# Graph attention: the quarter of the messages that ScalarE weighed is weighed by GpSimd, in the queue that gathers

## The chip, the cores and the metric

The kernel runs on one core of a Trainium2 chip. The metric is the device time of one execution in microseconds (us). TensorE is called PE here (PEld is its loading of weights), VectorE DVE, ScalarE ACT, GpSimd POOL and SyncE SP, as in the profile.

## The reference, cut to what matters

The program is a two-layer graph network over 3125 nodes with 256 features and 53125 edges sorted by their target node. The change touches the first layer's graph attention alone (8 heads of 32 columns):

```python
q = (x @ Wq + bq).reshape(n, H, C)
k = (x @ Wk + bk).reshape(n, H, C)
v = (x @ Wv + bv).reshape(n, H, C)
alpha = jnp.einsum('ehc,ehc->eh', q[dst], k[src]) / jnp.sqrt(jnp.float32(C))
amax = jax.ops.segment_max(alpha, dst, num_segments=n)
ex = jnp.exp(alpha - amax[dst])
denom = jax.ops.segment_sum(ex, dst, num_segments=n)
attn = ex / denom[dst]
msg = (v[src] * attn[:, :, None]).reshape(-1, H * C)
out = jax.ops.segment_sum(msg, dst, num_segments=n)
```

The kernel sums `v[src] * ex` and `ex` by target and divides later. The multiplication of the 256 columns of v[src] by their head's ex is what is called weighing below.

## The kernel before

`attention` (L887) walks over 440 steps (T1) of 128 edges each. Four steps are a half (Q4), two steps a pair (the code says duo), eight a unit U, sixteen a batch (B16); there are 110 halves and 27.5 batches. All targets of a step lie in one block of 128 nodes, so sums by target are matmuls with a one-hot matrix. The engines run their own queues, written out by hand, and meet at semaphores. Every queue is in order: what stands behind a wait waits as well.

**POOL (L943 to L952)** gathers the k and v rows of each step, 128 rows of 2 KB from `kv_tab` in DRAM, into the ring `kv`, which has 32 slots (RING * Q4), two batches. Before the gather of step t it waits until PE has summed step t - 32 (`summed`), whose slot it overwrites, and until DVE has multiplied about up to step t - 12 (`multiplied`).

**PE (`fetch`, L1057; `attend`, L1076)** spreads the targets' q rows over the edges of a pair (L1072, bf16, six matmuls) and counts `asked`. `attend` sums a pair: one matmul with zeros clears the second bank (L1083), then it waits for the one-hot of the half (`built`) and for the half's weighing, and multiplies (L1097, two f32 passes for each step, so four records a pair); each step counts `summed`. In a batch it also transposes scores and maxima (L1119, L1130) and makes small matmuls for the state carried from batch to batch (L1124, L1127, L1133). The order in the loop over batches (L1105 on) is fixed: pairs 1 to 8 of the batch before lie among the q matmuls of the coming one, and the transposition of the scores is behind all eight.

**DVE (L1135 on)** multiplies q by the gathered k rows (L1154, 128x512 for a pair), reduces by head (L1161, a half), adds the sums of a pair to the accumulator (L1181), and runs the segmented maximum by scans (L1243 to L1261). It ends a batch's scores with a subtraction of the maxima (L1267, `diffed`), which releases ACT's exponentials. It weighs three halves of each batch, 0, 1 and 3, at L1170 with one multiplication of 128x1024 each:

```python
v.tensor_tensor(rows, rows, wide(kv[:, slot(hh), 2 * D:2 * D + H1].unsqueeze(3), [P, Q4, H1, HD]),
                ALU.mult).then_inc(weighted, 1)
```

Its order around the place in question is add of pair 4, multiply, weighing of half 3, **add of pair 5**, reduction, add of pair 6, two multiplications, reduction, adds of pairs 7 and 8, scans, and the subtraction at L1267.

**ACT (L978 on)** makes the one-hot matrices: `node_hot` in bf16 for the q matmuls (L991, L994) and `edge_hot` in f32 for the sums (four times L1010, then L1015, counted by `built`). In a batch it first exponentiates (L1036, four times L1040, counted by `exped`), then in this order: `edge_hot` of half 1, weighing of steps 0 and 1 of half 2, `node_hot`, weighing of steps 2 and 3 of half 2, `edge_hot` of half 2, `node_hot`, `edge_hot` of half 3, `node_hot`, `edge_hot` of the next half 0, `node_hot`. The weighing is `weigh` (L1017 to L1026): one activation with a scale by partition for each step and head, 32 of 128x32 for a half (L1025). PE waits for it before pairs 5 and 6, by `weighed`.

**SP** loads the rows of targets and the flags.

Of the kernel before, what the change touches and what calls it, by code (L numbers as in the profile page):

```python
# [10 lines left out]
ALU = mybir.AluOpType  # L11
ACT = mybir.ActivationFunctionType
AX = mybir.AxisListType

P = 128
N = 3125
D = 256
# [12 lines left out]
T1 = C1 + NB - 1  # L30
G1 = (T1 + P - 1) // P
H1 = 8
# [67 lines left out]
def wide(ap, shape):  # L100
    return ap.to_broadcast(shape)
# [779 lines left out]
Q4 = U // 2  # L881
B16 = 2 * U
RING = 8
# [3 lines left out]
def attention(nc, k, e, q_parts, kv_tab, acc):  # L887
# [3 lines left out]
    HD = D // H1  # L891
    W = D + H1
    SCALE = float(HD ** -0.5)
    halves, duos = T1 // Q4, T1 // 2
    batches = -(-T1 // B16)
    NHOT, NEDGE, NROW = 4, 3, 4
    with Scope(nc) as s:
        kv = s.sb("at_kv", [P, RING * Q4, 2 * D + H1])
# [35 lines left out]
        weighed = s.sem("at_weighed")  # L934

        def slot(hh):
            return slice(hh % RING * Q4, hh % RING * Q4 + Q4)

        def halves_of(j):
            return list(range(4 * j, min(4 * j + 4, halves))) if 0 <= j < batches else []  # L940

        with nc.Block(no_gpsimd_drain=True) as block:
            @block.gpsimd  # L943
            def _(pool):
                for t in range(T1):
                    if t >= RING * Q4:
                        pool.wait_ge(summed, t - RING * Q4 + 1)
                    if t >= AHEAD + 2:
                        pool.wait_ge(multiplied, (t - AHEAD) // 2)
                    nc.gpsimd.indirect_dma_start(  # L950
                        out=kv[:, t % (RING * Q4), 0:2 * D], out_offset=None, in_=kv_tab,
                        in_offset=bass.IndirectOffsetOnAxis(ap=e.src[:, t:t + 1], axis=0)).then_inc(got[t // Q4 % RING], 16)  # L952

            @block.sync
            def _(sp):
# [22 lines left out]
            @block.scalar  # L978
            def _(act):
                a = nc.scalar.activation  # L980
                made = [0]

                def node_hot(hh):
                    if hh >= halves:
                        return
                    act.wait_ge(rowed[hh // 2 % (NROW // 2)], 16 * (hh // NROW + 1))
                    if hh:
                        act.wait_ge(hotted, hh)
                    if hh >= NHOT:
                        act.wait_ge(asked, 2 * (hh - NHOT) + 2)  # L990
                    a(away_n[:, :], rel_row[:, hh % NROW, :], ACT.Abs, bias=k.neg_col[:, :]).then_inc(away, 1)  # L991
                    made[0] += 1
                    act.wait_ge(away, made[0])
                    a(hot_n[:, hh % NHOT, :], away_n[:, :], ACT.Relu, bias=k.ones[:, 0:1], scale=-1.0).then_inc(hotted, 1)  # L994

                def first(j):
                    if j >= batches:
                        return
                    act.wait_ge(hotted, 4 * j + 1)
                    if j >= 3:  # L1000
                        act.wait_ge(rescaled, j - 2)
                    a(first_hot[:, j % 2:j % 2 + 1], hot_n[:, 4 * j % NHOT, 0:1], ACT.Copy).then_inc(firsted, 1)

                def edge_hot(hh):
                    if hh >= halves:
                        return
                    if hh:
                        act.wait_ge(built, hh)
                    for u in range(Q4):
                        a(away_e[:, u, :], k.count_row[:, 0:P], ACT.Abs, bias=e.rel[:, hh * Q4 + u:hh * Q4 + u + 1], scale=-1.0).then_inc(away, 1)  # L1010
                    made[0] += Q4
                    act.wait_ge(away, made[0])
                    if hh >= NEDGE:
                        act.wait_ge(summed, (hh - NEDGE + 1) * Q4)
                    a(hot_e[:, hh % NEDGE], away_e[:, :, :], ACT.Relu, bias=k.ones[:, 0:1], scale=-1.0).then_inc(built, 1)  # L1015

                def weigh(j, us):  # L1017
                    hh = 4 * j + 2
                    if hh >= halves:
                        return  # L1020
                    act.wait_ge(exped, hh + 1)
                    for u in us:
                        for h in range(H1):
                            row = kv[:, hh % RING * Q4 + u, D + h * HD:D + (h + 1) * HD]
                            ins = a(row, row, ACT.Copy, scale=kv[:, hh % RING * Q4 + u, 2 * D + h:2 * D + h + 1])  # L1025
                        ins.then_inc(weighed, 1)  # L1026

                for x in range(4):
                    node_hot(x)
                edge_hot(0)  # L1030
                for x in range(4, 8):
                    node_hot(x)
                for j in range(batches):
                    if j:
                        act.wait_ge(fell, j)
                        a(fade[:, j % 2:j % 2 + 1], fall[:, j % 2:j % 2 + 1], ACT.Exp, scale=SCALE).then_inc(faded, 1)  # L1036
                    act.wait_ge(diffed, j + 1)
                    for x, hh in enumerate(halves_of(j)):
                        act.wait_ge(got[hh % RING], 16 * Q4 * (hh // RING + 1))
                        a(kv[:, slot(hh), 2 * D:W + D], below[:, x * Q4:(x + 1) * Q4, :], ACT.Exp, scale=SCALE).then_inc(exped, 1)  # L1040
                    first(j + 1)
                    edge_hot(4 * j + 1)
                    weigh(j, (0, 1))
                    node_hot(4 * j + 8)
                    weigh(j, (2, 3))
                    edge_hot(4 * j + 2)
                    node_hot(4 * j + 9)
                    edge_hot(4 * j + 3)
                    node_hot(4 * j + 10)
                    edge_hot(4 * j + 4)  # L1050
                    node_hot(4 * j + 11)

            @block.tensor
            def _(pe):
# [21 lines left out]
                def attend(j, *xs):  # L1076
                    for x in xs:
                        p = j * U + x
                        if j < 0 or p >= duos:
                            continue  # L1080
                        if p >= 2:
                            pe.wait_ge(added, p - 1)
                        nc.tensor.matmul(ps_a[p % 2][:, 1, 0:W], nothing[:, 0:P], nothing[:, :], start=True, stop=False, skip_group_check=True)  # L1083
                        pe.wait_ge(built, p // 2 + 1)
                        if p // 2 % 4 == 2:
                            pe.wait_ge(weighed, Q4 * (p // 8 + 1))
                        else:
                            pe.wait_ge(weighted, p // 8 * 3 + (0, 1, 0, 2)[p // 2 % 4] + 1)
                        for u in range(2):
                            t = 2 * p + u  # L1090
                            if u == 0:
                                to = ps_a[p % 2][:, 0, 0:W]
                            else:
                                r = nc.s_assert_within(where[p // Q4][U + p % Q4], 0, 1,
                                                       skip_runtime_bounds_check_because="a step's block is its neighbour's or the next one")
                                to = ps_a[p % 2][:, ds(r, 1), 0:W].rearrange("p a w -> p (a w)")
                            nc.tensor.matmul(to, hot_e[:, t // Q4 % NEDGE, t % Q4, :], kv[:, t % (RING * Q4), D:2 * D + H1],  # L1097
                                             start=(u == 0), stop=(u == 1), skip_group_check=True).then_inc(summed, 1)
                        if p % Q4 == Q4 - 1:
                            del where[p // Q4]  # L1100
# [2139 lines left out]
def program(nc, a, out):  # L3240
    with Scope(nc) as s:
# [12 lines left out]
        with Scope(nc) as g:  # L3254
            e1 = Graph(g, "e1_", G1, streamed=True)
            with Scope(nc) as t:
                q_parts = t.sb("q_parts", [P, NB, 3, D], BF)
                with Scope(nc) as t2:
                    pj = Projection(t2)
                    stats = LayerStats(nc, t2, k, "n0_")  # L3260
                    with Scope(nc) as t3:
                        ld = Loads(nc, t3, k, pj, a)
                        turn_weights(nc, k, pj, ld, stats)
                    stats.finish()
                    project0(nc, k, pj, q_parts, kv_tab, a["pairs"], e1)
                    mixer_matrix0(nc, k, pj)
                acc = t.sb("acc0", [P, NB + 1, D + H1])
                attention(nc, k, e1, q_parts, kv_tab, acc)
                stats = LayerStats(nc, t, k, "n1_")
                combine0(nc, k, acc, stats)  # L3270
                stats.finish()
# [98 lines left out]
```

## Time and profile before

| | |
|---|---|
| median of 3 runs | 3045.84 us (3045.73 to 3049.63) |
| the profiled execution, span from first to last instruction | 3371.4 us |
| busy in the span: PE, DVE, POOL, ACT | 72%, 60%, 49%, 46% |
| the attention's steady part | 330.4 to 1092.4 us, 26 batches |

The profiled execution has a time of its own: for it only the span is told, and that is 325.6 us longer than the median of the runs made without the profiler. So durations and their order are read from it, and sums are set against both numbers. Times in the trace's rows are in us from the span's start; "idle before, releaser" is the idle time of that engine right before an instruction and what ended it; "remote" is a release that the profile cannot place, "issue" is idle time for which it shows no wait. A row with x16 is sixteen instructions in a row.

### The profile page before, as it was taken

What the parts mean: (1) busy time and instruction counts of PE and PEld (TensorE: products, weight loads), DVE (VectorE), ACT (ScalarE), POOL (GpSimd) and SP (SyncE); (2) the same over time, 40 slices, a digit from 0 to 9 for tenths busy, and PEclk for the clock granted to TensorE, in tenths of its full rate; (3) what the DMA queues carried; (4) which work ended last, traced back from release to release, by engine and by line L of the source; (5) the groups of instructions that cost most, each with busy time, mean ns of one, the idle gap of its engine ahead of it and who ended that gap; (6) DMA issues with size and microseconds to landing.
All of it is one profiled execution on the core that took longest, in us unless ns stands there. A gap on an engine that the chain in (4) does not pass through costs nothing. (4 is left out here: it accounts for less than half of the span.)

```text
span 3371.4 us, 41737 instructions
## 1 busy us (share of the span) xinstructions
PE 2414.5 (72%) x11076; PEld 1563.8 (46%) x11076; DVE 2015.5 (60%) x4071; ACT 1542.2 (46%) x4616; POOL 1637.9 (49%) x1754
## 2 busy tenths in 40 slices
PE   4995667766766656699855477777787777888785
PEld 2553444444444445556423122222226666666674
DVE  4564777777777888500183488888884622222377
ACT  0222767776766344311241488877883111112132
POOL 1644555555554204566673666666632066666300
PEclk8996888887878855599976698988898688888888
DMA  3214655555554012133230333333311211111104
GB/s 95 55 38 129 173 173 165 168 164 156 170 161 139 1 52 84 34 104 90 66 87 24 94 91 89 89 90 91 91 55 16 55 27 33 33 26 33 23 1 163
DMA packets 165630, 289.13 MB, mean 86 GB/s; under 512 B 55933, under 2 KB 99970, under 8 KB 165407
## 3 DMA queue, kind: packets, MB, share of 16 engines
q0 software_dynamic: 79344, 187.14, 20.5%
q1 hardware_dynamic: 73906, 80.60, 7.9%
q10 hardware_dynamic: 12156, 18.72, 1.6%
q8 instruction: 102, 1.67, 0.2%
q14 instruction: 122, 0.99, 0.1%
HBM read 250.08 MB, written 36.25 MB: 85 GB/s over the span
## 5 line engine op out<-in xcount | busy, mean ns | idle before, releaser
L2370 PE MATMUL cv_ps<-cv_msg,cv_hot 128*128 128x512 f32 x880 | 482.7, 689 | 194.0 <-remote 89.6
L950 POOL DMA_INDIRECT at_kv<-kv_tab,e_src x440 | 428.2, 973 | 386.2 <-PE at_a L1097 208.9
L2357 POOL DMA_INDIRECT cv_x<-x_tab,e_src x440 | 425.5, 967 | 227.8 <-issue 100.6
L2383 ACT ACTIVATE cv_msg<-cv_x,factors 128x64 f32<-128x64 f32 x1320 | 373.6, 335 | 104.1 <-issue 103.5
L2806 POOL DMA_INDIRECT gs_h<-h_tab,fc_q x312 | 294.3, 943 | 253.0 <-issue 86.6
L2370 PEld LDWEIGHTS cv_ps<-cv_msg,cv_hot 128*128 128x128 f32 x880 | 173.2, 214 | 503.1 <-issue 216.4
L2425 DVE TENSOR_TENSOR acc<-acc,cv_ps 128x256 f32 x880 | 315.6, 417 | 130.2 <-PE cv_ps L2370 76.8
L2021 POOL DMA_INDIRECT pairs<-gating_pair,gating_place x281 | 275.3, 980 | 206.5 <-issue 76.1
L1097 PE MATMUL at_a<-at_kv,at_hot_e 128*128 128x264 f32 x880 | 277.0, 447 | 47.7 <-issue 31.0
L1072 PE MATMUL at_q<-q_parts,at_hot_n 128*128 x1320 | 238.7, 340 | 52.2 <-DVE at_kv L1154 28.0
L2763 ACT ACTIVATE gs_x_hid<-gs_x_h,x_b 128x128 f32<-128x128 f32 x320 | 89.6, 373 | 376.6 <-remote 241.4
L2381 ACT ACTIVATE cv_msg<-cv_x,factors 128x256 f32<-128x256 f32 x440 | 217.9, 495 | 91.9 <-DMA cv_x<-x_tab,e_src 56.6
L1181 DVE TENSOR_TENSOR acc<-acc,at_a 128x528 f32 x220 | 154.5, 702 | 171.3 <-remote 78.0
L2740 PE MATMUL gs_x_y<-x_w,gs_x_hid 128*128 128x256 f32 x640 | 186.1, 441 | 69.5 <-ACT gs_x_hid L2763 46.5
L1097 PEld LDWEIGHTS at_a<-at_kv,at_hot_e 128*128 128x128 f32 x880 | 175.3, 221 | 89.1 <-issue 42.9
L1072 PEld LDWEIGHTS at_q<-q_parts,at_hot_n 128*128 128x128 bf16 x1320 | 154.1, 118 | 129.6 <-issue 77.0
L1025 ACT ACTIVATE at_kv<-at_kv 128x32 f32<-128x32 f32 x864 | 188.1, 306 | 0.0
L2740 PEld LDWEIGHTS gs_x_y<-x_w,gs_x_hid 128*128 128x128 f32 x640 | 133.9, 220 | 99.0 <-ACT gs_x_hid L2763 58.7
L2730 PE MATMUL gs_x_h<-xnT,x_w 128*128 128x128 f32 x1280 | 170.0, 290 | 6.8 <-issue 6.5
L2730 PEld LDWEIGHTS gs_x_h<-xnT,x_w 128*128 128x128 f32 x1280 | 166.1, 205 | 10.4 <-issue 6.7
L1154 DVE TENSOR_TENSOR at_kv<-at_kv,at_q 128x512 f32<-128x512 f32 x220 | 147.3, 680 | 27.2 <-remote 13.1
L2875 DVE TENSOR_SCALAR gs_hot<-gs_b,count_col 128x1024 bf16<-128x1024 f32 x39 | 50.1, 1284 | 162.3 <-PE gs_b L2845 88.1
(547 smaller groups left out, 4542.2 us busy)
## 6 DMA issues: line engine op xcount, KB each, us to landing
x_space<-in_L_ffn_w SPq DMA_DIRECT2D x16, 1024.0 KB
at_rel_row<-e_rel_rows SPq DMA_DIRECT2D x55, 256.0 KB
experts_out<-gs_y ACTq DMA_DIRECT2D x20, 512.0 KB
x_y<-experts_out SPq DMA_DIRECT2D x20, 512.0 KB, 6.9
at_kv<-kv_tab,e_src POOLq DMA_INDIRECT x440
cv_x<-x_tab,e_src POOLq DMA_INDIRECT x440
kv_tab<-p_qkv SPq DMA_DIRECT2D x25, 256.0 KB, 2.0
gs_h<-h_tab,fc_q POOLq DMA_INDIRECT x312
```

Source lines behind the costliest of these rows:

```text
L950: nc.gpsimd.indirect_dma_start(out=kv[:, t % (RING * Q4), 0:2 * D], out_offset=None, in_=kv_tab, in_offset=bass.IndirectOffsetOnAxis(ap=e. ...
L1072: ins = nc.tensor.matmul(ps_q[dd % 3][:, u, :], hot_n[:, t // Q4 % NHOT, t % Q4 * P:(t % Q4 + 1) * P], q_parts[:, ds(b, 1), n, :].rearrang ...
L1097: nc.tensor.matmul(to, hot_e[:, t // Q4 % NEDGE, t % Q4, :], kv[:, t % (RING * Q4), D:2 * D + H1], start=(u == 0), stop=(u == 1), skip_gro ...
L2021: nc.gpsimd.indirect_dma_start(out=pairs, out_offset=bass.IndirectOffsetOnAxis(ap=place_i[:, c:c + 1], axis=0), in_=pair[:, c, :], in_offs ...
L2357: nc.gpsimd.indirect_dma_start(out=xg[:, i % RT, u, :], out_offset=None, in_=x_tab, in_offset=bass.IndirectOffsetOnAxis(ap=e.src[:, t:t + ...
L2370: nc.tensor.matmul(ps[u % R][:, :], hot[:, i % 2, u, :], msg[:, i % 2, u, :], start=True, stop=True).then_inc(summed, 1)
L2381: nc.scalar.activation(msg[:, h, u, 0:D], xg[:, i % RT, u, :], ACT.Copy, scale=factor[:, t:t + 1, 0])
L2383: ins = nc.scalar.activation(msg[:, h, u, D + m * M:D + (m + 1) * M], xg[:, i % RT, u, 0:M], ACT.Copy, scale=factor[:, t:t + 1, 1 + m])
L2425: v.tensor_tensor(row, row, ps[u % R][:, n * D:(n + 1) * D], ALU.add).then_inc(added, 1)
L2730: ins = self.nc.tensor.matmul(self.ps_h[e % 2][:, f * P:(f + 1) * P], self.x1.w1[:, e, c, f * P:(f + 1) * P], self.xnT[:, c, b * P:(b + 1) ...
L2740: ins = self.nc.tensor.matmul(self.ps_y[e % 2][:, 0:D], self.hid[:, e % 2, f, :], self.x1.w2[:, e, f, :], start=(f == 0), stop=(f == FX // ...
L2806: nc.gpsimd.indirect_dma_start(out=hg[:, i % RT, u, :], out_offset=None, in_=h_tab, in_offset=bass.IndirectOffsetOnAxis(ap=e.src[:, i * U ...
```

## The change

ACT's `weigh` and its two calls go. POOL gets one, which weighs half 2 of batch j (hh = 4j + 2) with one multiplication of 128x1024 in the form that DVE has at L1170. Its place in POOL's queue is right before the gather of step 16j + 40, which is the one that overwrites the first slot of half 2; the last two (j = 25 and 26) come after the loop. PE's wait counts one for the half where it counted four.

```diff
             @block.gpsimd
             def _(pool):
+                def weigh(j):
+                    hh = 4 * j + 2
+                    if hh >= halves:
+                        return
+                    pool.wait_ge(exped, hh + 1)
+                    rows = kv[:, slot(hh), D:2 * D].rearrange("p u (h d) -> p u h d", d=HD)
+                    nc.gpsimd.tensor_tensor(rows, rows, wide(kv[:, slot(hh), 2 * D:2 * D + H1].unsqueeze(3), [P, Q4, H1, HD]),
+                                            ALU.mult).then_inc(weighed, 1)
                 for t in range(T1):
+                    if t >= 3 * B16 - 8 and (t + 8) % B16 == 0:
+                        weigh((t + 8) // B16 - 3)
                     if t >= RING * Q4:
                         pool.wait_ge(summed, t - RING * Q4 + 1)
...
+                for j in range((T1 + 7) // B16 - 2, batches):
+                    weigh(j)
...
-                def weigh(j, us):
-                    hh = 4 * j + 2
-                    if hh >= halves:
-                        return
-                    act.wait_ge(exped, hh + 1)
-                    for u in us:
-                        for h in range(H1):
-                            row = kv[:, hh % RING * Q4 + u, D + h * HD:D + (h + 1) * HD]
-                            ins = a(row, row, ACT.Copy, scale=kv[:, hh % RING * Q4 + u, 2 * D + h:2 * D + h + 1])
-                        ins.then_inc(weighed, 1)
...
                     edge_hot(4 * j + 1)
-                    weigh(j, (0, 1))
                     node_hot(4 * j + 8)
-                    weigh(j, (2, 3))
                     edge_hot(4 * j + 2)
...
                         if p // 2 % 4 == 2:
-                            pe.wait_ge(weighed, Q4 * (p // 8 + 1))
+                            pe.wait_ge(weighed, p // 8 + 1)
```

## Rows read from the trace of the kernel before

**Rows 1.** The page: span, and PE, its busiest engine (busy us, share, instructions).

```profile
span 3371.4 us, 41737 instructions
...
PE 2414.5 (72%) x11076; PEld 1563.8 (46%) x11076; DVE 2015.5 (60%) x4071; ACT 1542.2 (46%) x4616; POOL 1637.9 (49%) x1754
```

**Rows 2.** Busy time by window, the attention's 26 batches (us, then engines as named).

```profile
core 0: us, PE busy (x) PEld busy (x) DVE busy (x) ACT busy (x) POOL busy (x), PEclk, DMA share, GB/s
330.40:1092.40 762.00, 527.89 (x2484) 358.83 (x2482) 576.31 (x1037) 531.98 (x1712) 397.95 (x408) 0.81 0.57 163
```

**Rows 3.** List of waits, 330 to 1090 us (total us, times, longest us).

```profile
POOL at_kv L950 <- PE at_a L1097: 208.9, 95, 6.7
...
DVE acc L1181 <- remote: 78.0, 17, 6.2
...
DVE acc L1181 <- PE at_a L1097: 67.7, 65, 5.0
```

**Rows 4.** One line's instructions, L1267 (duration ns min/median/max, first and last start).

```profile
L1267 DVE TENSOR_TENSOR at_below<-at_score,at_t x28: 267/267/289, 330.4 to 1113.2; 128x128 f32<-128x128 f32 x28
```

**Rows 5.** Timeline of ACT, one batch (start us, us, what, idle before and releaser).

```profile
619.67 0.20 ACT L1036 ACTIVATE at_fade<-at_fall 8x1 f32<-8x1 f32 x1 [7.09 <-issue]
...
622.97 3.49 ACT L1025 ACTIVATE at_kv<-at_kv 128x32 f32<-128x32 f32 x16
...
627.73 3.48 ACT L1025 ACTIVATE at_kv<-at_kv 128x32 f32<-128x32 f32 x16
...
632.41 0.72 ACT L1015 ACTIVATE at_hot_e<-at_away_e,ones 128x512 f32<-128x512 f32 x1
```

**Rows 6.** Timeline of PE, the same batch, its fifth pair.

```profile
633.18 1.16 PE L1097 MATMUL at_a<-at_kv,at_hot_e 128*128 128x264 f32 x4 [1.60 <-issue]
```

**Rows 7.** Timeline of DVE, the same batch and the start of the next.

```profile
620.16 0.27 DVE L1267 TENSOR_TENSOR at_below<-at_score,at_t 128x128 f32<-128x128 f32 x1
...
631.46 1.22 DVE L1170 TENSOR_TENSOR at_kv<-at_kv 128x1024 f32<-128x1024 f32 x1
637.34 0.70 DVE L1181 TENSOR_TENSOR acc<-acc,at_a 128x528 f32 x1 [4.66 <-remote]
...
648.84 0.27 DVE L1267 TENSOR_TENSOR at_below<-at_score,at_t 128x128 f32<-128x128 f32 x1
```

**Rows 8.** Timelines of PE and DVE, the batch that starts at 473.3 us.

```profile
486.37 1.16 PE L1097 MATMUL at_a<-at_kv,at_hot_e 128*128 128x264 f32 x4 [1.56 <-issue]
...
487.67 0.70 DVE L1181 TENSOR_TENSOR acc<-acc,at_a 128x528 f32 x1 [1.78 <-PE at_a L1097]
...
497.62 0.70 DVE L1181 TENSOR_TENSOR acc<-acc,at_a 128x528 f32 x1 [4.73 <-remote]
```

**Rows 9.** Timeline of DVE, fifth additions of the batches at 330.4 and 1063.5 us.

```profile
345.06 0.70 DVE L1181 TENSOR_TENSOR acc<-acc,at_a 128x528 f32 x1 [1.45 <-PE at_a L1097]
...
1080.70 0.70 DVE L1181 TENSOR_TENSOR acc<-acc,at_a 128x528 f32 x1 [4.46 <-remote]
```

**Rows 10.** Groups of POOL's instructions by shape, whole span (busy us, mean ns, idle).

```profile
L1301 POOL TENSOR_TENSOR X<-X,c_bias 128x256 f32<-128x256 f32 x25 | 18.3, 742 | 70.9 <-ACT c_xn L595 70.8
...
L689 POOL TENSOR_TENSOR p_rest<-p_qkv,p_part 128x256 f32<-128x256 f32 x25 | 16.7, 670 | 2.0
...
L124 POOL MEMSET armed_dummy<- 128x1 f32 x1 | 0.1, 88 | 0.0
```

**Rows 11.** Timeline of POOL, the first, sixth and eighth gather of that batch.

```profile
625.78 0.94 POOL L950 DMA_INDIRECT at_kv<-kv_tab,e_src  x1 [5.78 <-PE at_a L1097]
...
632.03 1.47 POOL L950 DMA_INDIRECT at_kv<-kv_tab,e_src  x1 [0.30 <-issue]
...
635.05 0.95 POOL L950 DMA_INDIRECT at_kv<-kv_tab,e_src  x1 [0.30 <-issue]
```

**Rows 12.** Last full batch, first pair: PE's and DVE's timelines, and that window.

```profile
1095.63 2.10 PE L1097 MATMUL at_a<-at_kv,at_hot_e 128*128 128x264 f32 x4 [1.93 <-DVE at_kv L1170]
...
1097.93 0.70 DVE L1181 TENSOR_TENSOR acc<-acc,at_a 128x528 f32 x1 [0.19 <-PE at_a L1097]
...
1095.60:1097.70 2.10, 2.07 (x5) 1.50 (x6) 2.10 (x2) 2.10 (x11) 0.00 (x0) 0.50 0.00 0
```

## The prediction

> **What bounds the kernel now.** The page first: no engine is busy over 72% of the 3371.4 us span, so waits decide and the stage has to be read by itself [rows 1]. In the attention DVE, PE and ACT are each busy 69 to 76% of the time, POOL 52% [rows 2]. The list of waits says what holds whom: POOL waits 208.9 us for PE's summing matmuls, DVE's addition at L1181 waits 78.0 us for releases that the profile cannot place and 67.7 us for PE [rows 3]. So POOL sits behind PE, and DVE's only large idle time is before an addition.
>
> The step that starts a batch of 16 steps is the subtraction at L1267: 28 of them, from 330.4 to 1113.2 us [rows 4]. From the first to the twenty-seventh, 26 batches take 762.0 us [rows 2], 29.3 us each. I took one batch apart, 620.16 to 648.84 us, and give its times from its start. ACT exponentiates, builds half 1's one-hot and weighs from 2.8 to 6.2 and from 7.6 to 11.05 (two blocks of 16 activations, 3.49 and 3.48 us); only then it builds the one-hot of half 2, done at 12.97 [rows 5]. PE starts the fifth pair (the first of half 2) at 13.02 [rows 6]: ACT ends that wait. DVE adds it at 17.18, after 4.66 us idle [rows 7], and is then almost without a gap until the next L1267, 11.5 us later. **That is the cycle: front, fifth pair's sum, addition, 11.5 us of DVE tail.**
>
> PE's part of it is odd: 4.2 us lie between the fifth pair's matmuls and the addition. In the batch that starts at 473.3 us the same two are 1.3 us apart (486.37 to 487.67), and a delay of 4.73 us with an unplaced release stands at a later addition instead [rows 8]. So the unplaced wait wanders. I take it for a cost of recording PE. For this speaks that the profiled execution's span is 3371.4 us and the runs' median 3045.84 us, 325.6 us less; the stage's share of that by its length is 762/3371 of 325.6, 74 us, and bringing the addition from its mean place, 16.9 (over the 26 batches, whose first has it at 14.7 and whose last at 17.2 [rows 9]), to 14.3 in all of them takes 26 x 2.6 = 68 us. The batch of the timed runs would then be about 14.3 + 11.5 = 25.8 us.
>
> **The change, part by part.** *Removed from ACT:* 32 activations a batch, 6.97 us [rows 5], 864 in all. ACT then has half 2's one-hot at 12.97 - 6.97 = 6.0, too early to matter: DVE's own weighing of half 3 stands before the fifth addition and ends at 12.52 [rows 7]. After the tail ACT waits for DVE in any case (7.09 us before L1036 [rows 5]). By itself this removal would bring the fifth addition from 14.3 to about 12.5.
>
> *Added to POOL:* one multiplication of 128x1024 in each of 27 batches. No such instruction is in the trace. The nearest rows are POOL's multiplications and additions of 128x256, 670 to 742 ns [rows 10]; four times these is 2.7 to 3.0 us. Its smallest instructions take 0.1 us [rows 10], so with one fixed part of some 0.12 instead of four it is 4 x 0.58 + 0.12, or 2.4. I take 2.5, between the two and nearer to one fixed part; the range keeps 2.4 and 3.0, and 5.0 for the case that the operand repeated over each head's 32 columns doubles it, DVE's 1.22 for the same work being the lower end [rows 7]. The page GPSIMD Engine Reference of the Trainium skill (section Elementwise — side-by-side cycle accounting) has 4497 ns for 2048 elements, of which half is about 2.25 us: by it the sum below would be some 6 us smaller.
>
> *Moved: the place in POOL's queue.* This decides. weigh(j) stands right before the gather of step 16j+40, so behind the eight gathers of steps 16j+32 to 16j+39. The first of those overwrites the slot of step 16j and waits for PE's first sum of this batch; it starts at 5.6 after 5.78 us idle [rows 11]. The eight then follow each other 1.25 us apart (0.95 busy and 0.30 between), one of them 1.47 us long beside DVE's weighing of half 3; the last ends at 15.8 [rows 11]. The wait for exped is long over by then and costs nothing. POOL's multiplication starts at 15.8 + 0.3 = 16.1, somewhat sooner in batches without the long gather; I take 16.0, and its end at 18.5. ACT had finished the same work at 11.05.
>
> *The wait of PE* on weighed now ends at 18.5. PE's queue is in order: behind it stand pairs five to eight, the q matmuls and the transposition of the scores; DVE's queue behind the fifth addition holds two reductions and the subtraction at L1267. None can pass. PE has idled from about 11.5 by then. After an idle of 1.93 us in the last full batch the granted clock is 0.50 (its level of 1.2 GHz), PE takes 2.10 us over a pair and DVE adds 2.30 us after its start [rows 12], against 1.3 in the batch at 473.3 us [rows 8]. I take 2.3 and keep 1.3 for the range. The fifth addition comes at 18.5 + 2.3 = 20.8 in place of 14.3: **6.5 us a batch**.
>
> *What hides elsewhere.* The gathers behind the multiplication start with PE's sums at about 20.5; eight more take 10 us plus waits for L1154 and end before the next batch's 5.6. DVE multiplies their rows about 20 us later. Their delay costs nothing, and would cost only if it passed these 20 us. DVE is idle while POOL multiplies, so if the two hold each other up, it costs nothing. The tail of 11.5 us is DVE's and unchanged. Binding sizes: a batch is 14.3 + 11.5 before, 20.8 + 11.5 = 32.3 after.
>
> *The ends.* 26 batches have gathers ahead of weigh. In the last full one no gather is left; POOL can start at once, and the fifth addition comes up to 2 us sooner. Sum: 26 x 6.5 - 2 = 167 us. Against the runs' median this is 3045.8 + 167 = 3213. In the profiled execution's own time the addition moves from 16.9 to 20.8, so 26 x 3.9 - 2 = 99 us, and its span would go from 3371 to about 3470 if the unplaced wait does not come on top again.
>
> **The rivals.**
> 1. *The unplaced wait is real*, part of every run. Then only 99 us are added: 3145. For it: it sits at 17.2 in many batches alike. Against it: it wanders, and the median is 325.6 us shorter. Chance 0.2.
> 2. *POOL is slower than its rows say* (5.0 us). Then 26 x 2.5 = 65 us more: 3278. For it: an operand form that no row shows. Chance 0.07.
> 3. *Faster.* POOL's gathers are only so far apart under the profiler. The multiplication replaces ACT in time if 5.6 + 8p + 2.5 + 1.3 is at most 14.3, so p at most 0.61 us. The addition then falls to 12.5, held by DVE's weighing of half 3, and 26 x 1.8 = 47 us are gained: 2999. Against it: a gather is busy 0.94 us [rows 11], the pitch 1.25. Chance 0.05.
> 4. *No change:* the two sides of rival 3 cancel, at a pitch of about 0.6 to 0.7 us. 3046. Chance 0.03.
>
> **How the numbers follow.** My forecast has 0.65, and the time is its sum, rounded to 3210. Inside it the pitch may fall to the 0.95 of a busy gather (8 x 0.30 = 2.4 us less) and the clock stay high (1.0 less): 3.1 us a batch, 3125; with 3.0 us for POOL's multiplication it is 7.0 a batch, 3226. The range must take in rival 1 with a little of its own spread and leaves out rivals 2 to 4: 3105 to 3255. A change of 0.2%, 6 us, is about what a measurement of this kernel can tell. Slower by more has 0.65 + 0.2 + 0.07 = 0.92, within 0.03, faster 0.05.
>
> **What would show it.** In the profile after: a POOL multiplication of 128x1024, 27 times, of 2.4 to 3.0 us, starting about 16 us after L1267 and with no wait for ACT before it; PE's first matmul of the fifth pair right at its end, now released by POOL; DVE's idle time before L1181 up to some 7 us a batch; 32 us between subtractions at L1267; ACT about 44% busy in the stage; a lower granted clock around the fifth pair. Wrong would be: gathers closer than 0.7 us, a multiplication that starts before 11 us, or a batch still near 29 us in the profile.

## The result and the profile after

The changed kernel takes 3205.15 us (median of 4 runs, 3201.07 to 3207.06) against 3046.6 for the kernel before (4 runs, 3045.73 to 3049.63): 158.6 us more, a ratio of 1.0513 with a 95% interval of 1.0499 to 1.0526. The forecast was 3210.

The profiled execution of the changed kernel has a span of 3205.2 us, so here profile and clock agree. The one of the kernel before that the prediction read did not (3371.4 against 3046). The first experiment therefore profiled that kernel again; its span is 3046.4 us, and from here on it stands for the kernel before. Lines of the changed kernel are one lower than before behind the edit (L1267 is L1266).

The page of the changed kernel, span and busy times, to be held against [rows 1]:

```profile
span 3205.2 us, 40900 instructions
...
PE 2353.1 (73%) x11076; PEld 1565.5 (49%) x11076; DVE 2007.3 (63%) x4071; ACT 1337.2 (42%) x3752; POOL 1692.6 (53%) x1781
```

The same 26 batches by window, with the columns of [rows 2], in the changed kernel:

```profile
315.50:1145.90 830.40, 547.29 (x2493) 383.30 (x2490) 577.50 (x1038) 355.73 (x880) 454.69 (x440) 0.73 0.52 151
```

and the kernel before in its second profile:

```profile
317.10:992.90 675.80, 504.64 (x2493) 352.20 (x2491) 574.98 (x1037) 532.01 (x1712) 403.40 (x414) 0.82 0.63 186
```

These two rows hold nearly the whole result: 830.4 - 675.8 = 154.6 of the 158.6 us, 31.94 us a batch in place of 25.99. ACT lost a third of its work there (532 to 356 us), and the stage grew all the same. The granted clock of PE fell from 0.82 to 0.73.

The list of waits of the changed kernel, from 300 to 1200 us, tells who waits now:

```profile
DVE acc L1180 <- PE at_a L1096: 233.7, 94, 11.4
...
PE at_a L1096 <- POOL at_kv L951: 165.9, 26, 10.2
```

A chain of two: DVE waits for PE, and PE, once in each of 26 batches, for POOL's new multiplication. One line's view of that multiplication:

```profile
L951 POOL TENSOR_TENSOR at_kv<-at_kv x27: 1913/1924/1932, 333.4 to 1146.7; 128x1024 f32<-128x1024 f32 x27
```

The next rows are the timeline of one batch, the one that starts at 667.35 us. They show POOL's last gather before its multiplication, the multiplication, PE's fifth pair, DVE's fifth addition and the end of the batch.

```profile
667.35 0.27 DVE L1266 TENSOR_TENSOR at_below<-at_score,at_t 128x128 f32<-128x128 f32 x1
...
682.00 0.96 POOL L960 DMA_INDIRECT at_kv<-kv_tab,e_src  x1 [0.30 <-issue]
682.97 1.93 POOL L951 TENSOR_TENSOR at_kv<-at_kv 128x1024 f32<-128x1024 f32 x1
685.04 2.10 PE L1096 MATMUL at_a<-at_kv,at_hot_e 128*128 128x264 f32 x4 [5.34 <-POOL at_kv L951]
...
687.28 0.70 DVE L1180 TENSOR_TENSOR acc<-acc,at_a 128x528 f32 x1 [6.53 <-PE at_a L1096]
...
698.81 0.27 DVE L1266 TENSOR_TENSOR at_below<-at_score,at_t 128x128 f32<-128x128 f32 x1
```

The reader should see four things that touch end to end: the gather ends at 682.96, the multiplication fills 682.97 to 684.90, PE starts at 685.04, and DVE adds 2.24 us later after 6.53 us without work. From there to the next L1266 it is 11.53 us, about as long as before (11.5 us in the batch that the prediction read).

### The profile page after: what moved, and what is told of

Same layout as the page of the kernel before. It is cut to its first block and busy times, and to the rows that moved or that the text cites. A ratio compares the mean times of both kernels' runs of the same rounds, so it can differ in the third digit from the quotient of the medians.

```text
span 3205.2 us, 40900 instructions
## 1 busy us (share of the span) xinstructions
PE 2353.1 (73%) x11076; PEld 1565.5 (49%) x11076; DVE 2007.3 (63%) x4071; ACT 1337.2 (42%) x3752; POOL 1692.6 (53%) x1781
## 5 line engine op out<-in xcount | busy, mean ns | idle before, releaser
L2369 PE MATMUL cv_ps<-cv_msg,cv_hot 128*128 128x512 f32 x880 | 436.4, 639 | 140.8 <-DVE acc L2424 122.6
L1096 PE MATMUL at_a<-at_kv,at_hot_e 128*128 128x264 f32 x880 | 303.2, 481 | 170.9 <-POOL at_kv L951 165.9
L2369 PEld LDWEIGHTS cv_ps<-cv_msg,cv_hot 128*128 128x128 f32 x880 | 164.6, 200 | 412.2 <-ACT cv_msg L2382 242.3
L2382 ACT ACTIVATE cv_msg<-cv_x,factors 128x64 f32<-128x64 f32 x1320 | 356.4, 333 | 0.0
L2424 DVE TENSOR_TENSOR acc<-acc,cv_ps 128x256 f32 x880 | 306.9, 412 | 6.9 <-PE cv_ps L2369 4.1
L1096 PEld LDWEIGHTS at_a<-at_kv,at_hot_e 128*128 128x128 f32 x880 | 194.3, 244 | 222.6 <-issue 185.3
L2739 PE MATMUL gs_x_y<-x_w,gs_x_hid 128*128 128x256 f32 x640 | 170.4, 417 | 51.5 <-DVE gs_y L2769 50.9
L2882 DVE TENSOR_REDUCE gs_as_dst<-gs_d 128x32 f32<-128x96 f32 x39 | 10.0, 258 | 249.0 <-DMA gs_h<-h_tab,fc_q 249.0
L2729 PE MATMUL gs_x_h<-xnT,x_w 128*128 128x128 f32 x1280 | 162.9, 285 | 0.0
```

The source lines that it names most:

```text
L2369: nc.tensor.matmul(ps[u % R][:, :], hot[:, i % 2, u, :], msg[:, i % 2, u, :], start=True, stop=True).then_inc(summed, 1)
L2382: ins = nc.scalar.activation(msg[:, h, u, D + m * M:D + (m + 1) * M], xg[:, i % RT, u, 0:M], ACT.Copy, scale=factor[:, t:t + 1, 1 + m])
L2424: v.tensor_tensor(row, row, ps[u % R][:, n * D:(n + 1) * D], ALU.add).then_inc(added, 1)
L2729: ins = self.nc.tensor.matmul(self.ps_h[e % 2][:, f * P:(f + 1) * P], self.x1.w1[:, e, c, f * P:(f + 1) * P], self.xnT[:, c, b * P:(b + 1) ...
L2739: ins = self.nc.tensor.matmul(self.ps_y[e % 2][:, 0:D], self.hid[:, e % 2, f, :], self.x1.w2[:, e, f, :], start=(f == 0), stop=(f == FX // ...
```

## The experiments

Times from a batch's start are means over 25 batches of a kernel (the first is left out) and are worked out from the timelines; "addition" is the fifth addition of a batch. Besides the attention, the program has stages that no edit here touches: those behind it take between 2024.6 and 2038.0 us in the eleven profiles of the changed kernel and of the experiments. So where a difference of a few us matters, the stage is compared and not the whole time.

**The kernel before, once more.** No edit.

> The kernel before, unchanged, profiled once more. The recording theory (the unplaced wait before the fifth addition, mean place 16.9 us after L1267, belongs to that one profiled execution): span near the timed 3046 us, fifth addition at about 14.3 us after L1267, batch about 25.8 us. The rival (the wait is in every run): fifth addition again near 16.9 us and a batch of 29.3 us.

Measured: 3048.09 us (one run), span 3046.4, a batch of 25.99 us, the addition at 14.4. One of its batches, PE's fifth pair, DVE's addition and the batch's two ends:

```profile
628.84 0.27 DVE L1267 TENSOR_TENSOR at_below<-at_score,at_t 128x128 f32<-128x128 f32 x1
...
641.86 1.78 PE L1097 MATMUL at_a<-at_kv,at_hot_e 128*128 128x264 f32 x4 [1.18 <-ACT at_hot_e L1015]
...
643.78 0.70 DVE L1181 TENSOR_TENSOR acc<-acc,at_a 128x528 f32 x1 [2.02 <-PE at_a L1097]
...
655.49 0.27 DVE L1267 TENSOR_TENSOR at_below<-at_score,at_t 128x128 f32<-128x128 f32 x1
```

PE is released by ACT's one-hot, as [rows 5, 6] said, and no release is unplaced any more. In 20 of the 26 batches the addition follows PE's start by 1.30 us; in this one it is 1.92. So the 2.6 us before the addition belonged to that first execution. They are not the price of being profiled, though: this execution was profiled too. What disturbed the first one stays open.

**ACT's part alone.**

```diff
-                    weigh(j, (0, 1))
...
-                    weigh(j, (2, 3))
...
-                            pe.wait_ge(weighed, Q4 * (p // 8 + 1))
+                            pe.wait_ge(exped, p // 2 + 1)
```

> The kernel before without ACT's weighing of half 2 and nothing in its place (half 2's messages are left unweighed; PE waits for their exponentials instead). ACT theory (ACT's 32 activations set the fifth pair in the kernel before): fifth addition at about 12.5 us, held by DVE's weighing of half 3, 1.8 us a batch less, about 3000 us. Rival (ACT was covered and something else sets the batch): 3046 us as before. Against the early placement on the same chip it prices POOL's multiplication where it is hidden: under 10 us between them if it is hidden.

Half 2's messages stay unweighed in this kernel. Measured: 2986.9 us (ratio 0.981, 0.9788 to 0.9831), a batch of 23.84 us, the addition at 12.42, right behind DVE's weighing of half 3, with 0.01 us of idle time. ACT's activations did set the batch before, by 2.15 us. The change took away a real bound.

**The place, moved to the front.** weigh(j) stands before the gather of step 16j+32.

```diff
-                    if t >= 3 * B16 - 8 and (t + 8) % B16 == 0:
-                        weigh((t + 8) // B16 - 3)
+                    if t >= 2 * B16 and t % B16 == 0:
+                        weigh(t // B16 - 2)
...
-                for j in range((T1 + 7) // B16 - 2, batches):
+                for j in range((T1 - 1) // B16 - 1, batches):
```

> The changed kernel with weigh(j) moved ahead of the eight gathers of steps 16j+32 to 16j+39, where POOL is idle until PE's first sum. Queue theory (the place costs, not the instruction): the fifth addition waits only for DVE's own weighing of half 3, at about 12.5 us, batch about 24.2 us, time about 3000 us, below both kernels. Rival (POOL's multiplication costs wherever it stands, by holding up DVE's weighing of half 0 or the gathers by its 1.92 us or more): the time stays at 3050 us or above.

Measured: 2991.43 us, ratio to the kernel before 0.9824 (0.9801 to 0.9847), a batch of 23.84 us, the addition at 12.37. **This one beats both kernels**: the same instruction, the same engine, eight gathers earlier, and 214 us less than the changed kernel. It is within 5 us of the version without any weighing of half 2, so POOL's 1.92 us are hidden there. The 9 us below the expected time are the batch of 23.84 where 24.2 was expected (26 x 0.36). POOL's timeline shows that the margin is gone, however (in 25 batches it is never idle for over 0.4 us):

```profile
600.16 0.95 POOL L960 DMA_INDIRECT at_kv<-kv_tab,e_src  x1 [0.30 <-issue]
601.41 0.94 POOL L960 DMA_INDIRECT at_kv<-kv_tab,e_src  x1 [0.30 <-issue]
602.66 1.75 POOL L960 DMA_INDIRECT at_kv<-kv_tab,e_src  x1 [0.31 <-issue]
604.72 1.96 POOL L960 DMA_INDIRECT at_kv<-kv_tab,e_src  x1 [0.30 <-issue]
606.98 0.95 POOL L960 DMA_INDIRECT at_kv<-kv_tab,e_src  x1 [0.30 <-issue]
607.95 1.92 POOL L951 TENSOR_TENSOR at_kv<-at_kv 128x1024 f32<-128x1024 f32 x1
```

Nothing but the 0.30 us of issue lies between its instructions. The gathers of the batch before run into this one (started at 600.49) until 607.93, and two of them are stretched from 0.95 to 1.75 and 1.96 us. DVE's multiplications of two SBUF operands run from 602.38 and from 604.64, so each of the two gathers started while one of them was under way.

**The place, behind four gathers.** (t + 12) in place of (t + 8) above.

> The changed kernel with weigh(j) after four of the eight gathers. Queue theory: four gathers of 1.25 us fewer lie before it, so the fifth addition moves from 20.1 to about 15 us and the time falls by 26 x 5.0 = 130 us to about 3075 us. Rival (the cost of the instruction itself): a few us only, 3190 us or more.

Measured: 3028.31 us (0.9944, 0.9925 to 0.9962), a batch of 25.32 us. The direction was right, but the stage is 172 us shorter than in the changed kernel where 130 were expected. The multiplication starts at 10.37 instead of 15.85 (5.5 us, not 5.0), and PE's pair costs 1.27 us instead of 2.25 up to the addition, which comes at 13.71. What was missing in the expectation is the clock. Something new is in DVE's timeline, here with POOL's:

```profile
456.26 0.95 POOL L960 DMA_INDIRECT at_kv<-kv_tab,e_src  x1 [0.30 <-issue]
456.59 3.65 DVE L1169 TENSOR_TENSOR at_kv<-at_kv 128x1024 f32<-128x1024 f32 x1
457.22 1.93 POOL L951 TENSOR_TENSOR at_kv<-at_kv 128x1024 f32<-128x1024 f32 x1
```

DVE's weighing takes 3.65 us instead of 1.22 and ends at 460.24, 1.09 after POOL's multiplication. Over 25 batches this weighing has a mean of 2.08 us here, against 1.23 in the changed kernel.

**The place, behind six gathers.** (t + 10).

> The changed kernel with weigh(j) after six of the eight gathers. Queue theory: the multiplication starts 2 x 1.25 us earlier than behind all eight (15.85), at 13.35 us, so 26 x 2.5 = 65 us come off 3205, about 3140 us. With the clock theory on top: the shorter idle time of PE may keep the granted clock up for the fifth pair, which is 0.9 us a batch more, about 3117 us. Rival (steps of the gathers don't matter, only whether PE waits for POOL at all): as the changed kernel, 3205 us.

Measured: 3134.55 us (1.029, 1.0273 to 1.0307), a batch of 29.31 us, 68 us of stage time less than behind eight. Multiplication at 13.21, addition at 17.47; the clock stayed low (2.14 us from PE's start to the addition on the mean). The queue theory holds and the clock's hoped-for part does not come. With weigh behind eight, six and four gathers the batch is 31.94, 29.31 and 25.32 us.

**A small multiplication in the old place.** Only 32 columns of one step are multiplied:

```diff
-                    rows = kv[:, slot(hh), D:2 * D].rearrange("p u (h d) -> p u h d", d=HD)
-                    nc.gpsimd.tensor_tensor(rows, rows, wide(kv[:, slot(hh), 2 * D:2 * D + H1].unsqueeze(3), [P, Q4, H1, HD]),
+                    s0 = slot(hh).start
+                    rows = kv[:, s0:s0 + 1, D:D + HD].rearrange("p u (h d) -> p u h d", d=HD)
+                    nc.gpsimd.tensor_tensor(rows, rows, wide(kv[:, s0:s0 + 1, 2 * D:2 * D + 1].unsqueeze(3), [P, 1, 1, HD]),
```

> The changed kernel, same place in POOL's queue, but its multiplication covers one head of one step (128x32; the rest of half 2's messages is left unweighed). Queue theory: only the instruction's own 1.92 us shrinks, to some 0.1 to 0.2, so 26 x 1.8 = 47 us come off: about 3158 us, and the fifth addition stays behind the eight gathers at about 18.4 us after L1266. Rival (POOL's multiplication of 128x1024 is what made the change slow): the time returns to the 3046 us of the kernel before or below.

Measured: 3152.81 us (1.0354, 1.0337 to 1.0372); the small instruction takes 0.25 us:

```profile
L952 POOL TENSOR_TENSOR at_kv<-at_kv 128x32 f32<-128x32 f32 x27 | 6.8, 252 | 15.2 <-ACT at_kv L1042 14.8
```

It is 52 us less than the changed kernel, but 11 of these lie behind the attention, where the edit changes nothing. In the 26 batches (30.37 us each) 41 of the 154.6 us that the change cost go with the work of the instruction. The other 114 stay with hardly any multiplication at all: they are the wait in the queue and what it does to PE's clock.

**PE's clock kept up.** 48 more matmuls of zeros before the fifth pair:

```diff
-                        nc.tensor.matmul(ps_a[p % 2][:, 1, 0:W], nothing[:, 0:P], nothing[:, :], start=True, stop=False, skip_group_check=True)
+                        for _ in range(49 if p % 8 == 4 else 1):
+                            nc.tensor.matmul(ps_a[p % 2][:, 1, 0:W], nothing[:, 0:P], nothing[:, :], start=True, stop=False, skip_group_check=True)
```

> The changed kernel with 48 more matmuls of zeros ahead of the fifth pair, in PE's idle time, so that its clock does not fall before the pair (they end near 17 us, ahead of POOL's 17.8). Clock theory (2.3 us from PE's start to the addition instead of 1.3, because the granted clock is at 1.2 GHz): the fifth addition moves from 20.2 to about 19.2, 26 x 1.0 = 26 us less, about 3180 us. Rival (the clock has no part in the lengthened batch, or falls all the same): 3205 us, or more if the added matmuls hold up the pair.

Measured: 3171.81 us, 33 less than the changed kernel. The two kernels' windows around the fifth pair, first the changed one and then this one (the third number from the right is the granted clock):

```profile
683.00:687.00 4.00, 1.96 (x5) 1.39 (x6) 0.00 (x0) 0.00 (x0) 2.36 (x2) 0.50 0.56 182
```

```profile
646.10:647.20 1.10, 1.10 (x6) 0.88 (x7) 0.00 (x0) 0.00 (x0) 0.15 (x1) 1.00 0.40 151
```

At 1.00, the 2.4 GHz level, the addition follows PE's start by 1.27 us in 23 of 26 batches; in the changed kernel, at 0.50, by 2.25 in all 26. The batch is 1.0 us shorter, 30.93, so 26 of the 33 us are gained in the 26 batches, as many as expected. The last full batch is 4.4 us longer, because the added matmuls stand in PE's way where it does not wait for POOL, and the stages behind the attention happen to be 13 us shorter in this execution.

**POOL's multiplication twice, in the early place.** The second waits for the first; half 2 is weighed by the square.

```diff
+                    for x in range(2):
+                        nc.gpsimd.tensor_tensor(rows, rows, wide(kv[:, slot(hh), 2 * D:2 * D + H1].unsqueeze(3), [P, Q4, H1, HD]),
+                                                ALU.mult).then_inc(weighed, 1)
+                        pool.wait_ge(weighed, 2 * j + x + 1)
```

> The early placement with POOL's multiplication done twice (half 2 is weighed by the square). If POOL is full in the early placement (16 gathers and one multiplication take 23.8 us), each further 1.93 us lengthens the batch by as much: 26 x 1.95 = 50 us more than 2991, about 3041 us. If POOL still has slack and DVE alone sets the batch: within 10 us of 2991 us.

Measured: 3050.87 us (1.0017, 1.0006 to 1.0028), a batch of 26.21 us: 2.4 us more for 2.0 more of work, and 10 us above the expected time. At least a part of the rest is collisions: DVE's weighing of half 3 takes 1.66 us on the mean here instead of 1.22. POOL is full in the early placement. DVE, which alone would allow 23.84, and POOL meet there.

**Three engines.** The early placement, and ACT weighs half 3 in place of DVE:

```diff
                     edge_hot(4 * j + 1)
+                    act.wait_ge(exped, min(4 * j + 4, halves))
+                    scale3(j, (0, 1))
+                    edge_hot(4 * j + 2)
                     node_hot(4 * j + 8)
-                    edge_hot(4 * j + 2)
+                    scale3(j, (2, 3))
+                    edge_hot(4 * j + 3)
                     node_hot(4 * j + 9)
-                    edge_hot(4 * j + 3)
...
-                    weight(A, 3)
```

> The early placement, and ACT weighs half 3 in place of DVE (two blocks of 16 activations, ahead of the one-hots of halves 2 and 3). If DVE alone sets the 23.84 us batch of the early placement, 1.22 us less of DVE work gives about 22.9 us a batch (ACT's 15.3 us up to half 3's one-hot takes a part back), about 2965 us. If POOL, which has no wait of over 0.3 us left there, sets it: no gain beyond what fewer collisions with DVE's weighing give the gathers, 2980 to 2992 us.

Measured: 3027.47 us (0.9924, 0.9893 to 0.9954), worse than either expected. POOL's multiplication has slid forward to 1.66 us, to where DVE's first weighing stood; that it does so because POOL is no longer behind is likely, but not shown. POOL's and DVE's timelines in one batch:

```profile
518.62 0.27 DVE L1281 TENSOR_TENSOR at_below<-at_score,at_t 128x128 f32<-128x128 f32 x1
...
519.75 1.92 POOL L952 TENSOR_TENSOR at_kv<-at_kv 128x1024 f32<-128x1024 f32 x1
520.05 1.66 DVE L1208 SCALAR_TENSOR_TENSOR acc<-at_shrink,acc 128x8 f32 x1 [0.16 <-DVE at_shrink L1205]
...
521.97 1.21 DVE L1185 TENSOR_TENSOR at_kv<-at_kv 128x1024 f32<-128x1024 f32 x1
```

POOL ends at 521.67. What is held up beside it is a small DVE instruction of 8 columns (L1208), which ends at 521.71. On the mean it takes 1.62 us in this kernel, against 0.17 in the kernel before. DVE's weighing starts 3.35 us into the batch, where without POOL's multiplication beside it it starts at 1.89.

**The same, two gathers later** (t % B16 == 2).

> The three-engine version with POOL's multiplication two gathers later. In the version before, POOL's multiplication (1.66 to 3.58 us after the batch's start) stood across DVE's first weighing, whose start went from 1.89 to 3.33 us, and DVE's first addition from 6.1 to 7.1. Collision theory: moved to about 8 us, where DVE has no multiplication of two SBUF operands, it gives that 1.0 us a batch back: batch 24.4 us, 26 us less than 3027, about 3002 us. Rival (DVE's first weighing is late because ACT's exponentials or PE come later in this version): no change, 3027 us.

Measured: 2994.03 us (0.9826, 0.981 to 0.9843), a batch of 23.99 us. POOL now multiplies at 8.02, and DVE:

```profile
510.87 0.27 DVE L1281 TENSOR_TENSOR at_below<-at_score,at_t 128x128 f32<-128x128 f32 x1
...
512.75 1.25 DVE L1185 TENSOR_TENSOR at_kv<-at_kv 128x1024 f32<-128x1024 f32 x1
...
518.72 1.92 POOL L952 TENSOR_TENSOR at_kv<-at_kv 128x1024 f32<-128x1024 f32 x1
```

The collision was the cause and cost 1.4 us a batch. But taking 1.22 us of work from DVE gains nothing over the early placement: DVE now idles 1.12 us before the addition. PE's and DVE's timelines of this batch tell what holds it:

```profile
520.18 0.68 DVE L1169 TENSOR_TENSOR at_kv<-at_kv,at_q 128x512 f32<-128x512 f32 x1
...
521.11 0.90 PE L1085 MATMUL at_q<-q_parts,at_hot_n 128*128 x6 [0.47 <-DVE at_kv L1169]
...
521.96 1.05 PE L1112 MATMUL at_a<-at_kv,at_hot_e 128*128 128x264 f32 x4
...
523.16 0.70 DVE L1196 TENSOR_TENSOR acc<-acc,at_a 128x528 f32 x1 [1.08 <-PE at_a L1112]
```

DVE's multiplication by q releases PE's next q matmuls, and the fifth pair follows them without a wait. From that multiplication's start to the addition this path is 3.0 us long here. In the early placement the same two points are 3.0 us apart as well. There PE again goes from these q matmuls to the fifth pair without a wait, and DVE is busy the whole time: its own work and the path through PE are equally long, so shortening the first alone cannot help.

## Why the prediction was right

By its terms, each from a batch's start, beside what the changed kernel's trace shows:

- *The last of the eight gathers ends at 15.8*: 15.85. The pitch of 1.25 us held in an undisturbed execution, so rival 3 and rival 4 fall.
- *0.3 us between gather and multiplication*: about 0.01. Those 0.30 us precede a gather and not any instruction of POOL's. 0.3 too much; but 0.14 between the multiplication's end and PE's start had no term.
- *POOL's multiplication 2.5 us*: 1.92. This is the term that was mis-sized most, by 0.6 us, 15 us of the sum, and 1.92 lies outside the 2.4 to 3.0 us that were to be the sign of it in the profile. Four times the 128x256 rows less a fixed part of 0.12 was still too high: the 128x32 and 128x1024 forms of this operation take 0.25 and 1.92 us, so the fixed part is about 0.2 us and the slope 1.68 ns a column. The 2.25 us estimated from the page GPSIMD Engine Reference of the Trainium skill (section Elementwise — side-by-side cycle accounting; half of its 4497 ns) was nearer than the term and still above the trace. Rival 2 (5.0 us) falls.
- *2.3 us from PE's start to the addition because the clock is low*: 2.25. The experiment with added matmuls shows that it is the clock.
- *The addition at 20.8, before at 14.3*: 20.2 and 14.4. *The tail 11.5, unchanged*: 11.7 over the 26 batches, and 11.5 before. With PE's clock kept up it is 11.5 again, so the 0.2 belongs to the clock.
- *6.5 us a batch*: 5.95, so 154.6 for 169.
- *The last full batch gains up to 2 us*: wrong, and for two reasons. This batch takes 0.5 us more (21.37 for 20.87), and its fifth addition comes at 13.3. There were not 2 us to gain: in the kernel before, this batch has its fifth addition at 13.0 already and not at 14.4. And POOL multiplies at its very start, 1146.72 to 1148.63, and beside it DVE's instruction of 8 columns takes 1.37 us for 0.17, so that the first weighing starts only at 1148.92:

```profile
1145.88 0.27 DVE L1266 TENSOR_TENSOR at_below<-at_score,at_t 128x128 f32<-128x128 f32 x1
...
1146.72 1.91 POOL L951 TENSOR_TENSOR at_kv<-at_kv 128x1024 f32<-128x1024 f32 x1 [14.71 <-ACT at_kv L1041]
...
1147.29 1.37 DVE L1192 SCALAR_TENSOR_TENSOR acc<-at_shrink,acc 128x8 f32 x1 [0.16 <-DVE at_shrink L1189]
...
1148.92 1.21 DVE L1169 TENSOR_TENSOR at_kv<-at_kv 128x1024 f32<-128x1024 f32 x1
```

- *The unplaced wait is not part of the timed runs* (against rival 1, 3145 us): right, and the choice that made the forecast; with the batch of 29.3 us as base it would have been 60 us too low. The reason given, that recording PE costs it, was not: a profiled execution without it exists. The evidence that carried was the span against the median.
- *Nothing is paid for the gathers behind the multiplication, and nothing for DVE beside it*: right for the 26 batches. ACT at 43% of the stage was forecast at 44%.
- A slip of reading without consequence: ACT's first block of activations ends at 6.3 us and not at 6.2 (622.97 + 3.49 - 620.16 [rows 5]).

Sum: 154.6 us in the 26 batches, 0.5 in the last full one, and 3.5 outside them, where the change does nothing. The mechanism was right, but that 3210 came within 5 us of 3205.15 is in part luck: 14.4 us too much in the 26 batches stand against 2.5 too little in the last one, 3.5 outside and 3 of rounding.

## What to carry to other kernels

Work moved to an idle engine is done when that engine's queue comes to it, not when its inputs are ready: look at what stands ahead of it in the queue, and place it ahead of the wait that the engine spends idle. Here the same instruction cost 159 us behind eight gathers and gained 53 ahead of them. And before a sum is built on a trace, hold its span against the timed runs; where they differ, ask in which waits.

## What the runs showed of the hardware

- POOL and DVE hold each other up in both directions. Beside POOL's multiplication DVE's of 128x1024 went from 1.22 to as much as 3.65 us, and the 8-column instruction from 0.17 to 1.62 us on the mean of the first kernel with three engines. POOL's own mostly kept 1.91 to 1.93 us, but not always. With POOL's multiplication done twice, this is a batch in which the second one started right after DVE's:

```profile
613.29 1.22 DVE L1171 TENSOR_TENSOR at_kv<-at_kv 128x1024 f32<-128x1024 f32 x1
...
613.33 2.95 POOL L952 TENSOR_TENSOR at_kv<-at_kv 128x1024 f32<-128x1024 f32 x1
```

  The page SBUF — State Buffer of the Trainium skill (section Who interferes with whom) says that such a pair contends and that the one that starts first wins. These rows agree with both. In the row at 456.59 DVE started first and lost nevertheless; there a gather of POOL's was under way since 456.26, so the rule fits only if a gather holds DVE up too, which no run isolates.
- The same section of the Trainium skill infers that a tensor_tensor does not stall the writing of gathers' descriptors. The traces disagree: gathers that overlapped one took 1.75 and 1.96 us instead of 0.95, and [rows 11] have one of 1.47. In the early placement all 73 gathers of the attention that took over 1.1 us overlapped such a multiplication.
- One execution of the kernel before was 326 us longer than its runs, with waits whose release the profile cannot place (78.0 us before DVE's additions alone [rows 3]). The eleven later profiles, one of them of the same kernel, have no such wait.
